# Values of all heads projected at once, tokens on partitions, with the later heads' columns parked in DRAM

## The reference, cut to what matters

```python
h = layernorm(x)
q = h @ Wq.T                      # 16 heads x 128
k = h @ Wk.T                      # 4 heads x 128
v = h @ Wv.T                      # 4 heads x 128
q = elu(rope(q)) + 1;  k = elu(rope(k)) + 1
# per token: state += k (outer) v;  z += k;  out = (q @ state) / (q . z + 1e-6)
x1 = x + layernorm(out @ Wo.T)
g = silu(layernorm(x1) @ w_gate) * (layernorm(x1) @ w_up)
g = keep the two largest of every four of g
out = x1 + layernorm(g @ w_down)
```

## Time and profile before

| | |
|---|---|
| median of 3 runs | 1207.67 us (1207.64 to 1207.93) |
| the profiled execution | 1208.09 us |
| its span in the trace | 1206.3 us |
| PE busy | 1190.4 us (99%) |
| DVE, ACT, POOL busy | 746.4, 520.6, 502.5 us |
| granted TensorE clock over the span | 0.998 |

### The profile page before, as it was taken

How to read it: one execution, slowest core, us unless ns; L and a number is a source line. 1 busy time by engine, 2 the same in 40 slices (tenths; PEclk the granted TensorE clock), 3 DMA queues, 4 the chain that set the end, 5 groups by cost and what they waited for, 6 DMA issues and landing times.

```text
span 1206.3 us, 16031 instructions
## 1 busy us (share of the span) xinstructions
PE 1190.4 (99%) x6014; PEld 1005.2 (83%) x6014; DVE 746.4 (62%) x1283; ACT 520.6 (43%) x1013; POOL 502.5 (42%) x402
## 2 busy tenths in 40 slices
PE   8999999999999999999999999999999999999996
PEld 7788888888888888888888888888888888888885
DVE  8856554745565547565555376766666765555568
ACT  5554545444545445455445433433323342333322
POOL 6333523414446325254245444444425552434315
PEclk9999999999999999999999999999999999999999
DMA  6121312222425122233033322121203331212111
GB/s 214 53 78 46 104 45 65 71 50 71 122 62 139 54 71 80 70 79 79 18 91 112 104 79 71 53 70 39 67 10 100 111 96 44 61 44 61 45 44 70
DMA packets 49389, 88.74 MB, mean 74 GB/s; under 512 B 6304, under 2 KB 6560, under 8 KB 49312
## 3 DMA queue, kind: packets, MB, share of 16 engines
q1 hardware_dynamic: 49312, 87.71, 25.7%
HBM read 64.09 MB, written 8.39 MB: 60 GB/s over the span
## 4 chain that ended last, share of the span: by engine, by line
PE 94%; DVE 2%; POOL 1%; ACT 1%; DMA 1%; issue 1%; DVEq 0%; SPq 0%; POOLq 0%
PE bank_q L507 9%; PE bank_q L509 9%; PE bank_q L508 9%; PE bank_y L509 5%; PE bank_y L508 5%; PE bank_y L507 5%; PE bank_od L637 5%; PE bank_t L509 5%; PE bank_t L507 5%; PE bank_t L508 5%; PE bank_od L507 4%; PE bank_od L508 4%; PE bank_od L509 4%; PE bank_od L640 4%; PE bank_s L507 4%; PE bank_s L508 4%
## 5 line engine op out<-in xcount | busy, mean ns | idle before, releaser
L1268 POOL TENSOR_TENSOR w_lo<-stage,w_hi 128x512 fp32r<-128x512 f32 x96 | 130.3, 1373 | 152.7 <-ACT w_hi L808 152.7
L507 PE MATMUL bank_q<-x_hi,w_hi 128*128 128x512 f32 x436 | 174.7, 401 | 0.7 <-DVE scratch L1033 0.7
L509 PE MATMUL bank_q<-x_lo,w_hi 128*128 128x512 f32 x436 | 170.5, 391 | 0.0
L508 PE MATMUL bank_q<-x_hi,w_lo 128*128 128x512 f32 x436 | 169.9, 390 | 0.0
L1268 POOL TENSOR_TENSOR big_lo<-hidden,big_hi 128x512 fp32r<-128x512 f32 x30 | 69.0, 2319 | 188.6 <-ACT big_hi L931 188.6
L1268 POOL TENSOR_TENSOR big_lo<-q_rows,big_hi 128x1024 fp32r<-128x1024 f32 x31 | 80.8, 2608 | 108.2 <-ACT big_hi L852 108.2
L922 ACT ACTIVATE scratch<-hidden 128x512 f32<-128x512 f32 x64 | 40.6, 634 | 177.3 <-DVE hidden L1183 177.3
L1080 DVE TENSOR_SCALAR small<-bank_od 128x4 f32<-128x4 f32 x64 | 10.2, 159 | 157.3 <-PE bank_od L640 103.3
L509 PE MATMUL bank_y<-wout_lo,a_hi 128*128 128x512 f32 x256 | 100.0, 390 | 0.0
L508 PE MATMUL bank_y<-wout_hi,a_lo 128*128 128x512 f32 x256 | 99.8, 390 | 0.0
L507 PE MATMUL bank_y<-wout_hi,a_hi 128*128 128x512 f32 x256 | 99.8, 390 | 0.0
(11 more groups left out here) (329 smaller groups left out, 2977.6 us busy)
## 6 DMA issues: line engine op xcount, KB each, us to landing
q_rows<-scratch SPq DMA_DIRECT2D x116, 128.0 KB, 2.3
x_rows<-x SPq DMA_DIRECT2D x48, 256.0 KB, 3.1
stage<-wq SPq DMA_DIRECT2D x32, 256.0 KB, 2.8
stage<-wo SPq DMA_DIRECT2D x32, 256.0 KB, 2.7
stage<-wg SPq DMA_DIRECT2D x32, 256.0 KB, 2.8
stage<-wu SPq DMA_DIRECT2D x32, 256.0 KB, 2.9
stage<-wd SPq DMA_DIRECT2D x32, 256.0 KB, 2.6
x<-x_rows SPq DMA_DIRECT2D x16, 256.0 KB, 2.5
```

Source lines behind the costliest of these rows:

```text
L507: pe.matmul(ps, whi, xhi, start=first, stop=False, skip_group_check=True)
L508: pe.matmul(ps, wlo, xhi, start=False, stop=False, skip_group_check=True)
L509: return pe.matmul(ps, whi, xlo, start=False, stop=last, skip_group_check=True)
L1268: return pool.tensor_tensor(dst, full, hi.bitcast(F32), ALU.subtract)
```

## The change

The values of all four heads are now projected together, 128 tokens at a time, with the rows as the stationary operand and the four heads' value weights as the moving one. A projection is again 12 matmuls of 128x512, there are again 16 of them, and the result has tokens on partitions, so it isn't turned. ACT copies the first head's 128 columns into `Vr` and the other 384 into one of two buffers, from which a DMA stores them in DRAM (`store_values`); a DMA of 256 pieces of 512 bytes loads two chunks back when a later head needs them (`load_values`, 24 in all).

The places of the 16 projections move. `v_slot` was `4p - 3`, that is slots 1, 5, 9, ... 57 and one in the opening. It is now: two in the opening, slots 1 to 6, and slots 31 to 38. All four value weights are needed at once: those of batch 0 are split in the opening, those of batch 1 in slots 27 to 29, into parts of the buffers of the rows (`Xh`, `Xl`) that are free then; because of that the rows of batch 1 are turned later (`IN_1`).

Besides: in the opening the low part of query pair 0 moves from POOL to DVE, and DVE rotates pair 1 before it forms pair 0; two query weights move from the opening to slots 0 and 1; the last `query_split` (slot 59) goes ahead of the high part of the quotients.

```diff
-def v_slot(p):
-    return 4 * p - 3
+def v_slot(i):
+    b, c = i // TT, i % TT
+    return 31 + c if b else c - 1 if c > 1 else -1
...
-IN_1 = [3, 6, 7, 10, 11, 14, 15, 18]
+IN_1 = [7, 10, 11, 14, 15, 18, 19, 22]
...
+            def store_values(i):
+                g.wait_ge(act_v, i + 1)
+                sp.dma_start(v_rest[i // TT, i % TT, :, :], fresh[i % 2][:, P:W]).then_inc(st_v[i % 2], 16)
+
+            def load_values(p, part):
+                b, kv, c = p // 8, p // 2 % NU, p % 2 * 4 + 2 * part
+                last = 4 * p - (1 if part else 3)
+                g.wait_ge(pe_pv, last + 1)
+                g.wait_ge(pe_st, 7 * (last // 8) + min(last % 8 + 1, 7))
+                for i in (TT * b + c, TT * b + c + 1):
+                    g.wait_ge(st_v[i % 2], 16 * (i // 2 + 1))
+                rows = v_rest[b, c:c + 2, :, (kv - 1) * P:kv * P].rearrange("n t d -> t n d")
+                sp.dma_start(Vr[:, 2 * part:2 * part + 2, 0:P], rows).then_inc(ld_v[part], 16)
...
+                if kind == "a" and i < SLOTS and i % 4 == 0 and from_rows(i // 4):
+                    load_values(i // 4, 1)
+                if kind == "a" and i + 2 < SLOTS and i % 4 == 2 and from_rows(i // 4 + 1):
+                    load_values(i // 4 + 1, 0)
...
-            def values(p):
-                split_wait(g, ("v", p // 2, 0))
-                if p:
-                    g.wait_ge(dve_k1, p + 1)
-                project(value_bank(p)[:, :], 5, p // 8 * 2 + p % 2).then_inc(pe_v, 1)
-            def turn_values(p):
-                g.wait_ge(act_vt, p + 1)
-                g.wait_ge(dve_xl, turned[0])
-                for c in range(4):
-                    ins = pe.transpose(turned_values_bank(p)[:, c * P:(c + 1) * P], vT[:, c * P:(c + 1) * P], ident[:, :])
-                ins.then_inc(pe_vt, 1)
+            def values(i):
...
+                for kk in range(KT):
+                    split_wait(g, ("v", b, kk))
+                    wh, wl = dest(("v", b, kk))
+                    ins = three(value_bank(i), Xh[:, half, kk, t], Xl[:, half, kk, t], wh, wl, kk == 0, kk == KT - 1)
+                ins.then_inc(pe_v, 1)
+                made[0] += 1
...
-                if s % 4 == 0 and 0 < s < SLOTS:
-                    turn_values(s // 4)
...
-            def take_values(p):
-                g.wait_ge(pe_v, p + 1)
-                g.wait_ge(dve_kx, p + 1)
-                copy(vT, value_bank(p)[:, :]).then_inc(act_vt, 1)
-
-            def values_split(p):
-                g.wait_ge(pe_vt, p + 1)
-                g.wait_ge(pe_pv, 4 * p)
-                copy(Vr[:, :, 0:P], turned_values_bank(p)[:, :].rearrange("p (c d) -> p c d", c=4)).then_inc(act_vr, 1)
+            def take_values(i):
...
+                copy(Vr[:, c % 4, 0:P], value_bank(i)[:, 0:P])
+                copy(fresh[i % 2][:, P:W], value_bank(i)[:, P:W]).then_inc(act_v, 1)
...
+                if s == FREE + 1:
+                    query_split((s + 3) // 2)
...
+            rotate(1)
             query_sum(0)
-            rotate(1)
             rotate_keys(0)
             rotate_sum(1)
             key_sum(0)
+            g.wait_ge(act_qh, 1)
+            dve.tensor_tensor(big_l[:, 0, 0:2, :], pair_of(0)[3], big_h[:, 0, 0:2, :].bitcast(F32),
+                              ALU.subtract).then_inc(dve_fl, 1)
```

More of the change, by code:

```diff
@@ L26 @@
 LAST = SLOTS - 8
-OPEN = 12
+OPEN = 13
 EPS_LN = 1e-5
@@ L56, in k_slot, with value_at, from_rows, row_loads @@
     return 4 * p - 4
-def v_slot(p):
-    return 4 * p - 3
+def v_slot(i):
+    b, c = i // TT, i % TT
+    return 31 + c if b else c - 1 if c > 1 else -1
+def value_at(s):
+    return next((i for i in range(B * TT) if s >= 0 and v_slot(i) == s), None)
+def from_rows(p):
+    return p // 2 % NU > 0
+def row_loads(p):
+    return sum(from_rows(i) for i in range(p + 1))
 JOBS = [(kind, b, t) for kind, b in (("in", 0), ("in", 1), ("res", 0), ("mid", 0), ("res", 1), ("mid", 1),
@@ L113, in weight_plan @@
 def weight_plan():
-    plan = [(("q", 0, i), -1) for i in range(4)] + [(("k", 0, 0), -1), (("v", 0, 0), -1)]
-    plan += [(("o", 0, h), -1) for h in range(4)]
+    plan = [(("q", 0, i), -1) for i in range(4)] + [(("k", 0, 0), -1)]
+    plan += [(("v", 0, kk), -1) for kk in range(KT)] + [(("o", 0, h), -1) for h in range(4)]
     for u in range(1, UNITS + 1):
@@ L119, in weight_plan @@
         if more:
-            plan += [(("q", u, 0), (base - 1) if u > 1 else -1), (("q", u, 1), base if u > 1 else -1)]
+            plan += [(("q", u, 0), max(base - 1, 0)), (("q", u, 1), max(base, 1))]
         else:
@@ L225, in build @@
         rotk, xk, Ek, Sf, Tn = [scr[:, i, :] for i in range(8, 13)]
-        vT = rotk
+        fresh = [fresh_rows[:, i, :] for i in range(2)]
         def pair_of(j):
@@ L684, in slot_a @@
                     keys(p)
-                if 1 <= p < STEPS and s == v_slot(p):
-                    values(p)
+                if value_at(s) is not None:
+                    values(value_at(s))
                 if s % 4 != 3:
                     for job in jobs:
-                        g.wait_ge(act_vt, s // 4 + 2)
+                        g.wait_ge(dve_k1, s // 4 + 2)
                         turn(job)
@@ L778, in split_x @@
                 if job[0] == "mid":
-                    g.wait_ge(pe_v, 8 * job[1] + 7 + job[2] // 4)
+                    g.wait_ge(pe_q, 4 * (8 * job[1] + 6 + job[2] // 4) + 4)
+                if half in (1, 3) and job[1] + (job[0] == "mid") == 1:
+                    g.wait_ge(pe_v, TT * (B if half == 1 else 1))
                 copy(Xh[:, half, :, t * P:(t + 1) * P],
@@ L965, in _ @@
             query_split(1)
-            split(9)
-            values_split(0)
+            take_values(1)
+            for k in range(9, OPEN):
+                split(k)
             turned_split(0)
-            for k in range(10, OPEN):
-                split(k)
             for kind, i in TICKS:
@@ L1350, in _ @@
                 scaling(job)
-            for k in range(3, 8):
+            for k in range(3, 9):
                 split(k)
-            query_low(0)
-            g.wait_ge(dve_fl, 1)
-            for k in range(8, OPEN):
+            g.wait_ge(dve_fl, 2)
+            for k in range(9, OPEN):
                 split(k)
```

132 lines of the change are left out of this document (90 added, 42 removed).

## The result

The changed kernel took 1210.41 us (median, 1209.99 to 1210.77) against 1207.7 us for the kernel before beside it: a ratio of 1.0018, with a 95% interval of 1.0011 to 1.0025. (The two medians alone give 1.0022; 3 of the 16 executions of the kernel before took 1209.2 to 1210.4 us, and the ratio counts them.) The forecast was 1209.8 us. The span of the profiled execution is 1208.6 us, 2.3 longer than before (forecast 1208.4).

The account below looks back on a forecast made before the run. PE, busy 99% of the span, bounds the kernel: its own work and few waits count. -7.0 - 2.1 - 1.1 + 12.3 = +2.1 us gives a 1209.8 us median; forecast's own range 1208.2 to 1212.0, overall 1204.5 to 1213.5.

Parts of the forecast that it names:

- same: Whole kernel: a time of 1205.3 to 1210.1 us, within 0.2% of the kernel before; chance 0.34.
- slower: Whole kernel: slower than the kernel before by over 0.2%, 2.4 us; chance 0.47.
- Transposes: PE, ahead of the scores: 16 turns of values, four transposes each, go; 0.43 us a turn, 7.0 us less.
- The rival figure: The Trainium skill's 275 ns per transpose on PE: 64 would be worth 17.6 us, ending near 1199 us.
- Six waits: Slots 10, 18, 26, 42, 50, 58: PE waits for a_lo, then ACT's scalings; 2.05 us each, 12.3 us more.
- The opening: Before slot 1: PE's waits before the first scores and the queries behind them go; -2.1 us, bound -1.2.
- The wait that I did weigh: Opening: PE waiting 0.9 us for the second product of DVE's rotation of pair 1; taken as none.
- Slot 60: PE's wait before its scores shrinks to 0.8 us as the last query cast goes ahead; -1.1 us.
- (2): Slot 41 and its like: DVE's key rotation slips in before POOL's fourth low part; 5.2 us saved, 1204.6 us, 13%.
- (3): The six new PE waits do not come, as the chains have slack; 1197.5 us, 6%.
- (4): Scores at s % 4 == 0: low parts come late, half a microsecond of slip costs 3.4 us; 1213.2 us, 16%.
- (5): SP's queue: loads or stores delay the query pairs' DMAs beyond the margins, 5.6 us; 1215.4 us, 8%.

Follow-up runs that it names:

- turns_back: Changed kernel plus four never-read transposes of the identity ahead of the scores in slots 4, 8, ... 60 (15 groups); 1217.04 us.
- cover_back: Changed kernel plus twelve never-read matmuls behind the turn of the quotients in slots 9, 17, 25, 41, 49 and 57; 1214.91 us.
- den_first: Changed kernel with DVE's denominators and reciprocal ahead of the query pair's rotation in slots 10, 18, 26, 42, 50 and 58; 1207.86 us.
- no_value_wait: Changed kernel, but in the opening the projection of keys 1 no longer waits for ACT's copy of values 1; 1208.99 us.
- cast_back: Changed kernel with slot 59's cast of the last query pair behind the quotients' high part again; 1212.09 us.
- loads_twice: Changed kernel with each load of values, except the last step's, issued a second time on SP's queue (22 more DMAs of 128 KB); 1210.39 us.
- swap_k: Changed kernel with DVE's key-rotation product of two SBUF inputs ahead of the one that reads bank_t; 1208.50 us.

## Why the prediction was right

The measured 1210.41 us lies inside the forecast's own range, 1208.2 to 1212.0. It is 0.3 us above what the prediction counted as the same, while the ratio, 1.0018, is inside it: the result is on the edge between "same" (0.34) and "slower" (0.47).

**Transposes.** Forecast 0.43 us each. In each of 15 slots with s % 4 == 0 the distance from the state update to the scores had been 0.58 us; without the turn it is 0.14, 0.44 less (in slot 60 a wait hides it). turns_back, the other way round, gives 0.44 too. The rival figure is refuted as a price.

**Six waits.** Forecast 2.05 us each, in two parts: 1.2 before the scores and 0.84 before the turn. From the slot before each of these to the slot behind it PE's starts move by -2.75 + 1.99 us against the kernel before, and cover_back gives 16.5 - 4.5 = 12.0 us, 2.0 each. By distances in slot 42 the parts are 1.09 and 0.87 us. Place, whole and split were right. The chain named was right too, but not complete: at the turn PE also needs DVE's mask, which in slot 42 ended at 477.07, 0.59 us ahead of the scalings, and showed only once they were earlier (den_first).

**The opening** is the step that was mis-sized: -2.1 us forecast, with -1.2 as the bound. The prediction let PE be ready for the scores at 41.2, as if the new projection followed the one before. It came at 42.36, since keys 1 wait for ACT's copy of values 1, which cannot start before PE's product is out; that is 1.0 us in this execution, and no_value_wait gives 1.4 us back. At the first product of slot 1 PE was 1.24 us later than before (45.87 against 44.63), against 2.30 for a projection more and a turn less: the opening gave 1.06 us, less than the bound. The wait that I did weigh, for the second product of DVE's rotation, did not come. I had costed what DVE does there and had not asked what the new wait on `act_v` in `keys` costs: one copy on ACT, from PE's last product on.

Even of the 1.06 us not all is shown to be the change's. The first projection of queries starts at 11.78 us in the kernel before and at 11.31 in the changed one, and in the profiled executions of the experiments, which do not touch that stretch, anywhere from 11.0 to 12.2. So 0.47 of the 1.06 us can be chance. PE's waits ahead of 12 us, where this comes from, are not among the three places that the prediction names. No run puts the low part of pair 0 back on POOL or the rotation of pair 1 back in its place, so what each of these gave is open.

**Slot 60.** Forecast -1.1, with 0.8 us of wait left; measured 0.32 us left. PE is 4.05 us behind the kernel before at the scores of slot 59 and 2.28 at those of slot 60, of which 0.44 are the turn: -1.3. cast_back prices the reordered cast itself at 1.7 us.

The terms as measured, 6 x 1.99 - 15 x 0.44 - 0.43 - 1.06 - 1.33, add to 2.5 us against the span's 2.3; 0.2 us stay without a place. The forecast had 2.1. That it came so near is in part luck: of the 1.0 us missing in the opening, 0.4 was met by waits a little shorter than forecast and 0.2 by slot 60. The median is 0.6 us above the forecast's, the profiled execution 0.2, since the prediction put the median 0.4 us under the profiled execution, as before; now the two are equal (1210.41 and 1210.38).

**The rivals.** (2) DVE did not slip in: `L1128` took 1.60 us in all six slots, against 1.61 in the earlier trace rows. Its price was wrong too: where DVE did slip in with its order unchanged, in loads_twice, the chain was not 0.87 us shorter but 0.4 longer. (3) The waits came. (4) The low parts at s % 4 == 0 stayed ahead: the smallest distance fell from 0.65 to 0.22 us, by the 0.43 of the turn and no more. This is read from the trace; no run adds a slip there. (5) With nearly twice the loads the median stays, so the loads cost nothing that shows in it.

## What to carry to other kernels

Work on the bound engine that buys nothing may still be the cover under which other engines hand over. Before it is moved, read what was due behind it: each 2.75 us taken from behind the turn gave back 2.0, six times. When the cover has to go, look at the other engine's order before its load: a few swaps on DVE and ACT, with no work removed, won 9 of the 12 us back. Each swap showed the next thing in line (ACT's scalings, the mask, a_lo, the sum of outputs), so list everything that a waiting instruction needs, not only what ended last.

## What the runs showed of the hardware

A DVE operation with two SBUF inputs and a POOL operation that reads SBUF hold each other up in both directions: 0.74 us alone, 0.95 to 1.60 beside POOL, 1.06 and 1.58 for a sum of 0.69, and POOL's four operations 5.46 to 5.48 us in place of 5.03 when DVE gets between them. A DVE product with one input in PSUM kept its 0.68 us beside POOL. That is what the Trainium skill says ("SBUF — State Buffer", SBUF: two separate sides). What I had not expected is that the delay is passed on: getting in ahead of POOL's last operation shortened the chain by 0.35 us in swap_k, where the PSUM product stands between DVE's two SBUF operations, and made it 0.4 us longer in loads_twice, where they follow each other.

A matmul's row says how long it takes, not what it costs: transposes of 273 ns start 0.11 us apart, and a wait listed with 0.43 us of idle time costs 0.60 by distances.
